# The last group's gate exponentials: from ScalarE's Exp to a power on GpSimd

## What is computed

```
scores = softmax(x @ gate_w.T)                      # 8 experts
group_scores = scores.reshape(T, 4, 2).max(-1)      # 4 groups of 2
masked = where(scores' group is in the top 2 groups, scores, 0)
topk_w, topk_ids = top_k(masked, 2);  topk_w /= topk_w.sum(-1)
combine[t, topk_ids] = topk_w
gate, up = split(einsum('th,eih->tei', x, w13))
out = einsum('tei,ehi->th', silu(gate) * up * combine, w2)
```

## Time and profile before

| what | value |
|---|---|
| median of three runs (569.88 to 571.29) | 570.91 us |
| the profiled execution's own time | 570.1 us |
| its span | 568.3 us |
| TensorE matmul busy | 541.7 us (95%), 3954 instructions |
| VectorE busy | 294.2 us (52%), 875 |
| ScalarE busy | 243.3 us (43%), 560 |
| GpSimd busy | 167.9 us (30%), 152 |
| granted TensorE clock, mean | 0.987 |

### The profile page before, as it was taken

The page is one execution under the profiler, slowest core; times in us unless marked ns, Lnnn a source line. Parts: engine busy times, 40 slices in busy tenths (PEclk is TensorE's granted clock), DMA queues, the critical chain, the costliest instruction groups (busy, mean ns, idle before and its releaser), DMA issues.

```text
span 568.3 us, 11051 instructions
## 1 busy us (share of the span) xinstructions
PE 541.7 (95%) x3954; PEld 446.2 (79%) x3955; DVE 294.2 (52%) x875; ACT 243.3 (43%) x560; POOL 167.9 (30%) x152
## 2 busy tenths in 40 slices
PE   9999999999999999999999789969999999999991
PEld 8788878866555777768676679869999999999991
DVE  6748778888454867757688866721111111111110
ACT  1333665362356777787777233212222222222220
POOL 3102000113123242242220132443354544445332
PEclk9999999999999999999999999988999999999997
DMA  9920000001010000301623757776888888888721
GB/s 328 393 107 1 2 1 1 1 1 38 0 38 1 2 2 2 112 2 60 249 103 88 296 191 242 192 217 176 214 254 225 247 241 230 259 211 256 192 28 18
DMA packets 28507, 74.15 MB, mean 130 GB/s; under 512 B 5584, under 2 KB 20176, under 8 KB 23216
## 3 DMA queue, kind: packets, MB, share of 16 engines
q1 hardware_dynamic: 14368, 57.66, 28.4%
q0 software_dynamic: 7488, 10.39, 10.9%
q10 hardware_dynamic: 6608, 5.54, 3.0%
HBM read 62.86 MB, written 10.72 MB: 129 GB/s over the span
## 4 chain that ended last, share of the span: by engine, by line
PE 78%; DMA 6%; DVE 6%; ACT 3%; issue 3%; DVEq 1%; POOL 1%; POOLq 0%; ACTq 0%
PE ps L858 55%; PE ps L1150 9%; PE ps L862 9%; DMA out_x<-arena,row_no 5%; PE ps L1011 1%; DMA keep<-normed,row_no 1%; PE ps L1002 1%; PE ps L1014 1%; ACT ring L587 1%; PE ps L942 1%; POOL keep L384 1%; DVE mx L1649 1%; PE ps L1005 1%; PE ps L985 1%; DVE heads_out L1663 1%
## 5 line engine op out<-in xcount | busy, mean ns | idle before, releaser
L858 PE MATMUL ps<-keep,arena 128*128 128x128 f32 (+2 forms) x976 | 114.5, 274 | 0.2
L858 PEld LDWEIGHTS ps<-keep,arena 128*128 128x128 f32 x976 | 112.4, 192 | 1.6 <-DVE arena L1583 0.8
L1958 DVE TENSOR_TENSOR keep<-keep,ps 128x512 f32<-128x512 f32 x39 | 26.8, 688 | 150.8 <-PE ps L858 137.4
L392 POOL DMA_INDIRECT out_x<-arena,row_no x39 | 61.5, 1576 | 112.4 <-ACT arena L638 89.0
L1150 PE MATMUL ps<-arena,keep 128*128 x312 | 73.9, 380 | 1.2 <-issue 1.2
L356 POOL TENSOR_TENSOR ring<-arena,keep 128x512 f32<-128x512 f32 x32 | 33.2, 1039 | 103.6 <-PE ps L858 98.5
L1150 PEld LDWEIGHTS ps<-arena,keep 128*128 128x128 f32 x312 | 56.3, 190 | 7.8 <-issue 1.7
L627 ACT COPY keep<-ps 128x256 f32<-128x256 f32 x39 | 14.5, 371 | 101.4 <-PE ps L862 101.4
L587 ACT ACTIVATE ring<-ps,mx 128x128 f32<-128x128 f32 x192 | 52.1, 404 | 7.1 <-DVE mx L1649 4.6
L858 PE MATMUL ps<-ring,arena 128*32 128x128 f32 (+1 forms) x640 | 53.5, 349 | 0.9 <-ACT ring L594 0.8
L858 PE MATMUL ps<-arena,keep 128*128 128x256 f32 (+1 forms) x144 | 44.1, 455 | 0.3 <-ACT arena L559 0.3
(11 more groups left out here) (259 smaller groups left out, 809.3 us busy)
## 6 DMA issues: line engine op xcount, KB each, us to landing
arena<-in_w SPq DMA_DIRECT2D x29, 1024.0 KB
w_first<-in_w SPq DMA_DIRECT2D x10, 1024.0 KB
arena<-in_w SPq DMA_DIRECT2D x8, 512.0 KB, 7.1
keep<-in_keep SPq DMA_DIRECT2D x1, 3099.0 KB, 21.0
ring<-in_fold SPq DMA_DIRECT2D x1, 2112.0 KB, 12.4
arena<-in_x SPq DMA_DIRECT2D x4, 512.0 KB, 10.4
arena<-in_ctxT SPq DMA_DIRECT2D x4, 512.0 KB, 7.5
out_x<-arena ACTq DMA_DIRECT2D x4, 512.0 KB, 3.2
```

What stands on the lines that cost most here:

```text
L392: pool.indirect_dma_start(out=out_d, out_offset=bass.IndirectOffsetOnAxis(ap=row_no[:, t:t + 1], axis=0), in_=YO[t % DEEP], in_offset=None ...
L858: ins = pe.matmul(out, w, m, start=(k == 0), stop=(k == len(pairs) - 1))
L1958: dve.tensor_tensor(HA[r % 2], HA[r % 2], ps[:, 2 * (r % 2) + 1, :], ALU.mult).then_inc(act_ok, 1)
```

## The change

GpSimd sets a tile `exp_base` to e at the start and, between fetch(5) and fetch(6), raises it to the last group's 128x32 differences. It signals `g_exp` in ScalarE's place. ScalarE's third `exp_gate` goes; the first two stay as they are.

```diff
+        exp_base = sb("exp_base", [P, GB * NE])
...
+            def exp_last():
+
+                pool.wait_ge(g_diff, NG - 1)
+                pool.tensor_tensor(prob[:, B - GB:B], exp_base[:, :].rearrange("p (b e) -> p b e", b=GB), prob[:, B - GB:B], ALU.pow).then_inc(g_exp, 1)
...
             pool.memset(minus_half[:, :], -0.5).then_inc(half_set, 1)
+            pool.memset(exp_base[:, :], float(np.e))
             pool.wait_ge(half_set, 1)
             pool.memset(blank[:, :], 0.0).then_inc(blank_set, 1)
...
             fetch(5)
+            exp_last()
             fetch(6)
             add(0)
...
             turned(0, 2)
             answer(0, 0)
-            exp_gate(B - GB, B)
             turned(0, 3)
             gate(0, 2)
             store(3)
```

## The result

The changed kernel takes 575.58 us (median of four runs, 574.92 to 576.1), the kernel before 570.75 (569.88 to 571.29). The ratio is 1.0083, with a 95% interval of 1.0071 to 1.0096: slower, by 4.8 us. The forecast was 576.2.

A forecast was written before the change was run, and what follows sets the result against it. TensorE's wait for fetch(9)'s rows was taken as the bound, each microsecond at turn_in(9) costing one of kernel time. The profiled 570.1 plus 5.7, plus half the 0.8 median offset, gave 576.2 us; range 570.3 to 578.4.

The forecast's parts named there:

- the late ranks: On VectorE, the last route_softmax 4.8 us later, moving `picks` from 349.05 to 353.85.
- TensorE's wait at count(1): TensorE reaches count(1) at 349.74 and waits 4.1 us there for VectorE's late picks.
- the clock's fall behind it: After count(1)'s wait, exceeding 3.0 us, TensorE's clock falls, costing 2.7 us; chance 0.38 within the forecast's 0.60.
- removal on ScalarE: Dropping two table loads and an exponential, 2.8 us in all beside busy TensorE, gains nothing.
- power T: Length of GpSimd's 128x32 power from 339.86: 7.5 us, 0.1 plus 0.23 us for each of 32 elements.
- add(2) late by: In GpSimd's queue, add(2) waits for the late answer(2) and goes at 363.7 instead of 357.99: 5.7 us late.
- add(2) to fetch(9): GpSimd's queue takes 17.25 us for this stretch, the same as before the change.
- the in-between: Rival: GpSimd's power takes 1.6 to 4 us and mostly only the adds slip; 570.5 to 573 us, chance 0.07.
- the cheap power: Rival: GpSimd's power takes only 1.1 us, fetch(6) stays, no change; 570.2 to 571.0 us, chance 0.20.
- The lock-out: Rival: GpSimd's power blocks VectorE's two-input instructions, 1.0 us more; 577.2 us, or 571.5 with a cheap power; chance 0.06.
- the collision of the adds: Rival: a later add(0) avoids store(3)'s traffic and lands sooner, shortening turn_in(9)'s wait; 566 us, chance 0.07.
- Its second half: With turn_in(9)'s wait under 3.0 us, TensorE's clock does not fall there, saving 2.7 us.

The follow-up runs named there:

- the fill: Fill matmuls on TensorE in place of a wait: four ahead of count(1) in the changed kernel, 573.62 us; eight ahead of turn_in(9) in the kernel before, 568.33 us.
- e8_no_exp: The kernel before without the last group's exponential and with nobody waiting for one: 571.04 us, ratio 1.0002.
- e1_queue: The kernel before with an added, unused 128x32 power on its own tiles between fetch(5) and fetch(6) in GpSimd's queue: 571.37 us, ratio 1.0005.
- the swap: fetch(9) moved ahead of add(5) in GpSimd's queue: 565.37 us on the kernel before, 569.3 us on the changed kernel.
- e2_vector_late: The kernel before with six unused 128x512 reductions on VectorE ahead of the last route_softmax: 575.59 us, ratio 1.0076.

## Why the prediction was right

The direction and the path held: the late ranks, TensorE's wait at count(1), the clock's fall behind it, the late answer(2) and so the late add(2) and fetch(9). The profile has the signs too, the ScalarE table loads among them (8 instead of 10). That the size came out so near (5.7 us forecast in the sum, 4.8 measured) is partly luck: several terms were off and partly cancelled. By its own steps, times of after less 0.75:

| step | predicted | measured |
|---|---|---|
| removal on ScalarE | 0 | 0 (571.04 without the exponential) |
| power T | 7.5 us | 5.46 |
| softmax late by | 4.8 | 2.7 |
| TensorE's wait at count(1) | 4.1 | 2.05 |
| clock's price behind it | 2.7 | 1.7 in the trace (2.0 of kernel time by the fill) |
| down(2) starting later behind count(1) | not in the sum | 0.5 |
| answer(2) late by | 6.8 | 4.3 |
| add(2) late by | 5.7 | 3.2 |
| add(2) to fetch(9) | 17.25 | 21.2 |
| fetch(9) to turn_in(9) | 5.8 | 3.3 |
| turn_in(9) late by | 5.7 | 4.7 |
| turn_in(9) and gate_up(8) at the lower clock | as before | 0.3 shorter |

**The term that was mis-sized first is T.** "The other 0.93 us are the power's own arithmetic on four elements" took the whole 1.03 us, less a memset, as going by elements. The fixed part is 0.4 us, four times a memset's, and so 32 elements take 5.4 us and not 7.5. One size in a trace can't tell a slope from an offset; the memset was the wrong stand-in for the power's start. That is 2.1 us too much on the softmax and on the wait. The measured 5.46 us lies where the forecast and its rivals had nothing, between the in-between (up to 4) and 7.5.

**With T right, the forecast's own steps would have missed.** A power of 5.4 us makes the wait at count(1) 2.0 us, and the forecast let the clock fall only for a wait above 3.0. Without the fall answer(2) would have ended 2 us late, before the landing of add(1), and add(2) would have gone at about 359.8, 1.8 us late. The sum would have been 570.1 + 1.8 + 0.4 = 572.3, which is 3.3 below the measured time. The power that was put too long brought in the clock's fall, which came for a wait of half that length. This is the luck in the forecast.

**The second is the stretch from add(2) to fetch(9)**, which I carried over unchanged from one trace. It grew by 4.0 us: adds 3 and 4 were 7.3 and 6.2 us from issue to the next instead of 4.6 and 6.1, and add(3) came 5.9 after add(2) instead of 4.7. The rows of tile 9 then came 2.5 us quicker than before. Both in one, from add(2) to turn_in(9), are 24.55 us against 23.1: 1.45 us more than the sum had. Most of that (0.95 us) stands in e8_no_exp too, which has neither a power nor a late TensorE. What it comes from stays open.

**The clock** fell as forecast, but not for the reason given. The forecast said that a wait of 4.1 us exceeds the 3.0 after which it fell before; the wait was 2.05 and it fell all the same. In the traces here waits of 0.66, 0.92 and 1.45 us did not bring it down, and those of 1.89, 2.05 and 4.37 did.

Of the rivals: the cheap power falls with T. The lock-out falls: in the trace after, VectorE's two-input instruction of the pick of tile 2 ran in 0.16 us inside the power (at 341.34), as long as before, and the pick ended 1.40 us after the differences' start, against 1.31 in the kernel before. The rule of the Trainium skill (SBUF — State Buffer, Who interferes with whom), that such a pair locks each other out for the whole instruction, is again not what a power shows. Of the collision of the adds one half is borne out: with fetch(6) 3.9 us late add(1) followed add(0) 3.3 us sooner, and e1_queue lost nothing. But it gained nothing either, so as a way to a faster kernel it falls; that store(3) is what add(0) collides with was not tried. Its second half, that a wait below 3.0 us keeps the clock, is too wide: at turn_in(9) it held for 0.92 (the swap) and 1.45 (the fill), at count(1) 1.89 was enough for the fall.

## What to carry to other kernels

Before moving work off an engine, check that its time there is worth something: here ScalarE's 2.8 us stood in front of nothing, which the kernel without the exponential shows. A result that three engines wait for in turn (VectorE for the softmax, TensorE for the ranks, GpSimd for the answers) needs the engine with the shortest latency, not the idlest; here 5.5 us on an idle engine cost 4.8 of kernel time, and 2.9 us there cost nothing. A stretch that one trace shows once can be the lucky one: compare it over several runs before carrying it into a sum. And where the chain of waits runs through a queue in order, look for what stands ahead of the needed instruction for no reason: one exchanged line, fetch(9) ahead of add(5), was worth 5.8 us.

## What the runs showed of the hardware

- GpSimd's power (fp32) takes 0.4 us and 0.157 us an element a partition: 0.56, 1.66, 2.96 and 5.42 us for 1, 8, 16 and 32. A product of 512 elements takes 1.04 us on it, so an element of a power costs 80 times one of a product.
- TensorE's clock can fall after the wait is over. In the changed kernel it fell 1.3 us after work had begun again (1.0 in e2_vector_late), and held down(2) and part of gate_up(4) at the lower level for 3.4 us. A price of 1.7 us at turn_in(5), and of 2.0 in the kernel's time, thus came on top of a wait of 2.
- A timeline can shift as a whole from one run to the next: in four kernels with an unchanged start TensorE's first matmuls on loaded weights began 0.3 to 1.1 us later than in the kernel before.
- GpSimd's issue of an indirect add took 1.56 to 1.63 us in most rows, and 2.38 for add(3) after, with a bf16 instruction of VectorE inside it:

```profile
367.63 1.16 DVE L1927 TENSOR_TENSOR ring<-keep,routing 128x960 bf16<-128x960 f32 x1
368.87 0.47 DVE L1930 TENSOR_SCALAR ring<-ring,keep 128x960 bf16<-128x960 bf16 x1
```

In the kernel before, add(3) took 1.62 us, and that VectorE instruction (at 364.00, for 0.50 us) began 1.31 us after its start, 0.3 before its end:

```profile
362.69 1.62 POOL L392 DMA_INDIRECT out_x<-arena,row_no  x1 [0.53 <-issue]
```

In the other twelve traces it began 0.46 to 1.18 us after add(3)'s start, add(3) took 1.88 to 2.60 us, and each time add(3) ended 1.41 or 1.42 us after that instruction's start. A bf16 `TENSOR_TENSOR` of VectorE inside add(4) of the kernel before (367.30, for 0.66 us) left it at 1.59 us. The Trainium skill (SBUF — State Buffer, SBUF: two separate sides) says that VectorE in a two-port mode keeps GpSimd from writing descriptors. The traces fit that; which mode the instruction ran in no row shows, and it was not tried by itself.
